# Mixture-of-experts feed-forward on one core: own rows fetched apart from the gathers, one-hots in 16 bits, packed sizes, five visits, an end by block

## The reference, cut to what matters

```python
x_rot = cond(x)                          # gate and rotation, linear
top1 = argmax(softmax(x_rot @ router_w + router_b))
for i in range(8):
    a, g = split(x_rot @ w1[i] + b1[i])  # 256 -> 2 x 1024
    y = (a * sigmoid(g)) @ w2[i] + b2[i] # 1024 -> 256
    out = out + where(top1 == i, y, 0)
return x + out
```

## Time and profile before

| | us |
|---|---|
| median of 3 runs | 209.33 (209.0 to 209.66) |
| the profiled execution, its own time | 207.35 |
| its span, first to last instruction | 205.6 |
| mean granted TensorE clock | 0.994 of full |
| busy: PE, DVE, ACT, POOL | 191.6, 146.1, 125.1, 87.7 |
| moved by DMA | 42.34 MB |

### The profile page before, as it was taken

The page is one execution under the profiler, slowest core; times in us unless marked ns, Lnnn a source line. Parts: engine busy times, 40 slices in busy tenths (PEclk is TensorE's granted clock), DMA queues, the critical chain, the costliest instruction groups (busy, mean ns, idle before and its releaser), DMA issues.

```text
span 205.6 us, 4304 instructions
## 1 busy us (share of the span) xinstructions
PE 191.6 (93%) x1451; PEld 181.2 (88%) x1453; DVE 146.1 (71%) x296; ACT 125.1 (61%) x222; POOL 87.7 (43%) x138
## 2 busy tenths in 40 slices
PE   7997867999999999999999999999999999999960
PEld 3777733999999999999999999999999999999950
DVE  4928944678854888398869869995999488839510
ACT  2454770385756676486875958695777667648310
POOL 8002544631700645445467084555637364004403
PEclk9999999999999999999999999999999999999997
DMA  4999925879948161787198469618861976001001
GB/s 136 383 402 385 311 64 190 261 260 328 308 128 357 51 213 47 249 333 238 34 390 302 154 199 406 232 38 303 344 205 53 336 277 208 0 0 37 28 5 43
DMA packets 20054, 42.34 MB, mean 206 GB/s; under 512 B 2472, under 2 KB 14905, under 8 KB 17978
## 3 DMA queue, kind: packets, MB, share of 16 engines
q1 hardware_dynamic: 15808, 31.54, 42.8%
q0 software_dynamic: 4000, 10.50, 16.1%
q10 hardware_dynamic: 218, 0.01, 0.1%
HBM read 35.74 MB, written 8.13 MB: 213 GB/s over the span
## 4 chain that ended last, share of the span: by engine, by line
PE 90%; DMA 4%; issue 1%; DVE 1%; POOL 1%; ACT 1%; DVEq 0%; POOLq 0%
PE y_ps L1208 8%; PE g_ps L1176 8%; PE g_ps L1169 8%; PE a_ps L1169 8%; PE y_ps L1210 8%; PE a_ps L1176 8%; PE y_ps L1209 8%; PE a_ps L1172 8%; PE g_ps L1172 8%; PE y_ps L1120 3%; PE y_ps L942 3%; DMA x_turn<-x_rows,g_idx 2%; PE a_ps L1018 2%; PE a_ps L1099 2%; DMA x_rows<-arena 2%
## 5 line engine op out<-in xcount | busy, mean ns | idle before, releaser
L854 DVE SCALAR_TENSOR_TENSOR arena<-a_ps,b_t,arena 128x336 f32<-128x336 f32 (+1 forms) x64 | 33.3, 521 | 27.7 <-PE a_ps L1176 24.1
L579 ACT ACTIVATE arena<-g_ps,b_t 128x336 f32<-128x336 f32 (+1 forms) x64 | 32.2, 503 | 32.4 <-PE g_ps L1176 32.2
L452 POOL DMA_INDIRECT out_dram<-x_turn,s_idx x22 | 28.5, 1295 | 47.3 <-DVE x_turn L874 35.4
L740 DVE TENSOR_TENSOR w_lo<-w_raw,w_hi 128x1024 fp32r<-128x1024 f32 x32 | 37.7, 1221 | 9.1 <-DMA x_turn<-x_rows,g_idx 5.2
L438 POOL DMA_INDIRECT x_turn<-x_rows,g_idx x24 | 30.6, 1275 | 31.1 <-DMA out_dram<-x_turn,s_idx 17.3
L1208 PE MATMUL y_ps<-u_hi,w_hi 128*128 128x336 f32 (+2 forms) x128 | 38.1, 298 | 0.3 <-issue 0.3
L1210 PE MATMUL y_ps<-u_lo,w_hi 128*128 128x336 f32 (+2 forms) x128 | 37.5, 293 | 0.0
L1209 PE MATMUL y_ps<-u_hi,w_lo 128*128 128x336 f32 (+2 forms) x128 | 37.5, 293 | 0.0
L1169 PE MATMUL g_ps<-xr_hi,w_hi 128*128 128x336 f32 (+2 forms) x128 | 36.1, 299 | 0.0
L1169 PE MATMUL a_ps<-xr_hi,w_hi 128*128 128x336 f32 (+2 forms) x128 | 35.6, 294 | 0.0
L1172 PE MATMUL a_ps<-xr_hi,w_lo 128*128 128x336 f32 (+2 forms) x128 | 35.5, 293 | 0.0
(11 more groups left out here) (181 smaller groups left out, 306.8 us busy)
## 6 DMA issues: line engine op xcount, KB each, us to landing
w_raw<-in_L_ffn_w_dram SPq DMA_DIRECT2D x16, 1024.0 KB, 7.9
w_raw<-in_L_ffn_w_dram SPq DMA_DIRECT2D x16, 512.0 KB, 4.6
x_own<-in_x_dram SPq DMA_DIRECT2D x4, 512.0 KB, 6.0
x_rows<-x_own SPq DMA_DIRECT2D x4, 512.0 KB, 11.1
x_rows<-arena SPq DMA_DIRECT2D x8, 256.0 KB, 3.4
x_turn<-x_rows,g_idx POOLq DMA_INDIRECT x24, 6.0
out_dram<-x_turn,s_idx POOLq DMA_INDIRECT x22, 3.7
x_own<-x_rows,g_idx POOLq DMA_INDIRECT x8, 5.6
```

The lines of the kernel that those rows point to most:

```text
L579: nc.scalar.activation(sig[:, c % SIG_RING, 0:n], pair[c % RING][1][:, 0:n], ACT.Sigmoid, bias=b1_t[:, bass.ds(e * (2 * NC) + (NC + c), 1) ...
L740: V.tensor_tensor(unit_of(w1_lo, u), raw_unit(u), unit_of(w1_hi[:, :].bitcast(F32), u), ALU.subtract)\
L854: V.scalar_tensor_tensor(u32[:, c % (8 - SIG_RING), 0:n], pair[c % RING][0][:, 0:n], b1_t[:, bass.ds(e * (2 * NC) + c, 1)], sig[:, c % SIG ...
```

## The change

Six things are changed together.

- `x_rows` keeps only the rotated tokens (rows of 256 numbers). The four copies of `x` into it go. Each sub-tile is now filled by two indirect DMAs: `gather` takes the rotated row, and `fetch` takes the token's own row from the input. `gather(i+1)` no longer waits for the scatter of tile i-2; `fetch(i+1)` comes behind `scatter(i-1)` and has that wait.
- The slot one-hots are made by two 16-bit operations over 8 tokens each, with the token innermost, in place of 16 small ones; the token's number moves from them to the sub-tile one-hots, which take two operations each. POOL makes the table `steps16` for it.
- The sizes of all tiles lie in one word, `packed`, ready before `ctrl`; PE reads that word alone before the first tile.
- PE's order: the router's weights are turned behind f = 6, not f = 4; `rotate_blocks(2)` stands ahead of the wait for `in_row`; five visits in place of six, at other places.
- At the end PE turns back the first half of the features while ACT works on the second, whose first 128 columns come apart; the second half is turned back block by block into four banks, and DVE adds it so.
- DVE's first split of `w1` waits for the first gathered sub-tile, not for two.

```diff
-    x_rows = nc.dram_tensor("x_rows", (TOK, 2 * DIM), F32, kind="Internal").ap()
+    x_rows = nc.dram_tensor("x_rows", (TOK, DIM), F32, kind="Internal").ap()
@@ sync
-            for g in range(4):
-                sp.wait_ge(x_loaded[g], 16)
-                sp.dma_start(x_rows_v[:, 4 * g:4 * g + 4, DIM:ROW], x_tok[:, 4 * g:4 * g + 4, :]).then_inc(x_part_written, 16)
@@ gpsimd
+            nc.gpsimd.iota(steps16[:, :, :], pattern=[[1, P], [0, NB]], base=0, channel_multiplier=0,
+                           allow_small_or_imprecise_dtypes=True).then_inc(steps16_set, 1)
...
-                        out=pairs[buffer_of(i)][:, s * ROW:(s + 1) * ROW], out_offset=None, in_=x_rows,
+                        out=pairs[buffer_of(i)][:, s * ROW:s * ROW + DIM], out_offset=None, in_=x_rows,
...
+            def fetch(i):
+                for s in range(NSUB):
+                    nc.gpsimd.indirect_dma_start(
+                        out=pairs[buffer_of(i)][:, s * ROW + DIM:(s + 1) * ROW], out_offset=None, in_=x_flat,
+                        in_offset=bass.IndirectOffsetOnAxis(ap=g_idx[:, i * NSUB + s:i * NSUB + s + 1], axis=0),
+                        bounds_check=row_bound, oob_is_err=False).then_inc(fetched, 16)
...
             for i in range(NE):
                 wait_gathered(i)
                 if i + 1 < NE:
-                    if i + 1 >= YB:
-                        wait_scattered(i + 1 - YB)
                     gather(i + 1)
                 else:
                     nc.gpsimd.drain()
                 if i > 0:
                     scatter(i - 1)
                 else:
+                    fetch(0)
+                if i + 1 < NE:
+                    if i + 1 >= YB:
+                        wait_scattered(i + 1 - YB)
+                    wait_fetched(i)
+                    fetch(i + 1)
@@ scalar
                 if i >= NE - 1:
-                    for h in range(KH):
-                        biased(i, e, h, 0, FIRST, yt_done[h])
+                    biased(i, e, 0, 0, min(n, FIRST), yt_done[0])
+                    biased(i, e, 1, 0, P, yt_first)
+                    biased(i, e, 1, P, min(n, FIRST), yt_done[1])
@@ vector
+            def slot_one_hots(half):
+                tokens = slice(half * NB // 2, (half + 1) * NB // 2)
+                V.tensor_tensor(slot_oh[:, :, tokens], steps16[:, :, tokens],
+                                r_16[:, tokens].unsqueeze(1).to_broadcast([P, P, NB // 2]), ALU.is_equal).then_inc(slots_ready, 1)
...
+                link(V.tensor_tensor(to, steps16[:, first:first + count, :],
+                                     at[:, :].unsqueeze(1).to_broadcast([P, count, NB]), ALU.is_equal))
+                return V.tensor_tensor(to, to, tok_16[:, :].unsqueeze(1).to_broadcast([P, count, NB]), ALU.mult)
...
+            V.tensor_scalar(packed[:, :], left, float(len(SIZES) * sum(PLACES)), None, ALU.add).then_inc(packed_ready, 1)
...
+                V.tensor_tensor(rows[:, 0:blocks, 0], y_half[0][:, 0:blocks * P].rearrange("p (s d) -> p s d", d=P),
+                                rows[:, 0:blocks, 0], ALU.add)
+                for s in range(blocks):
+                    dve.wait_ge(block_turned, (i - NE + 1) * NSUB + s + 1)
+                    last = V.tensor_tensor(rows[:, s, 1], apart[s][:, 0:P], rows[:, s, 1], ALU.add)
...
-            for s in range(2):
-                dve.wait_ge(gathered[s], 16)
+            dve.wait_ge(gathered[0], 16)
@@ tensor
+            visit(2)
             keep_warm(early_ps, 5)
...
             rotate_blocks(1)
+            rotate_blocks(2)
+            visit(4)
             pe.wait_ge(consts_ready, CONSTS)
             pe.wait_ge(in_row_ready, 1)
...
-            visit(5)
             pe.wait_ge(still32_set, 1)
...
             last.then_inc(idx_spare_summed, 1)
+            visit(5)
             keep_warm_long(late_ps, 2)
-            pe.wait_ge(ctrl_ready, 1)
-            last_tile = load_last(pe)
-            visit(6)
-            keep_warm_long(late_ps, 2)
-            LANDING_AT = {(0, 7): 3, (1, 2): 4, (2, 3): 6}
+            pe.wait_ge(packed_ready, 1)
+            LANDING_AT = {(0, 2): 2, (1, 6): 4, (2, 1): 5}
+            LANDING_BEHIND = {0: 3}
...
-            turn_back_rows(NSUB)
+            pe.wait_ge(yt_done[0], at1)
+            for s in range(NSUB):
+                last = T.transpose(y_half[0][:, s * P:(s + 1) * P], yt[:, s * P:(s + 1) * P], ident[:, :])
+            last.then_inc(half_turned, 1)
+            for s in range(NSUB):
+                if s < 2:
+                    pe.wait_ge((yt_first, yt_done[1])[s], at1)
+                T.transpose(apart[s][:, 0:P], yt[:, ITEM + s * P:ITEM + (s + 1) * P], ident[:, :]).then_inc(block_turned, 1)
```

More of the change, by code:

```diff
@@ L55, in adaln_moe_ffn_kernel @@
     LEFT = 3
-    SPECIAL = len(SIZES)
+    PLACES = [1 << (LEFT * e) for e in range(NE)]
     EPS = 1e-8
@@ L105, in adaln_moe_ffn_kernel @@
         s_idx = sb("s_idx", TAB * NSUB, I32)
-        ctrl = sb("ctrl", 3 + TAB, I32)
+        ctrl = sb("ctrl", 2 + TAB, I32)
+        packed = sb("packed", 1, I32)
+        places = sb("places", NE)
         ident = sb("ident", P)
@@ L500, in _ @@
                         gather(i)
+                        fetch(i)
                         scatter(i)
@@ L833, in _ @@
             V.tensor_scalar(ctrl[:, 1 + NE:1 + TAB], owner, float(MORE), None, ALU.add)
-            V.memset(ctrl[:, 1 + TAB:2 + TAB], 0)
-            link(V.tensor_tensor(places[:, :], places[:, :], steps, ALU.mult))
-            link(V.tensor_reduce(left, places[:, :], AX.X, ALU.add))
-            V.tensor_scalar(ctrl[:, 2 + TAB:3 + TAB], left, float(SPECIAL << (LEFT * (NE - 1))), None, ALU.add)\
-                .then_inc(ctrl_ready, 1)
+            V.memset(ctrl[:, 1 + TAB:2 + TAB], 0).then_inc(ctrl_ready, 1)
             dve.wait_ge(idx_spare_summed, 1)
@@ L985, in _ @@
                 if f == 3:
-                    visit(2)
-                if f == 4:
+                    visit(3)
+                if f == 6:
                     pe.wait_ge(wr_loaded, 16)
@@ L1035, in _ @@
             T.matmul(xk_ps[1][:, NE:2 * NE], ones16[:, :], in_row[:, :], start=True, stop=True).then_inc(ranks_ready, 1)
-            for b in range(2, NB // 2):
+            for b in range(GROUPS - 1, NB // 2):
                 rotate_blocks(b)
-                if b == 5:
-                    visit(4)
             pe.wait_ge(b1_loaded, 16)
@@ L1233, in leaf, with jump, by_size @@
                 second_half(size, 1)
-            def by_size(size, low, high):
-                if low == high:
-                    if low == SPECIAL - 1:
-                        with pe.If(size >= SPECIAL):
-                            here = nc.cur_bb
-                            pe.br("special")
-                            nc.switch_bb("behind_special", parent=here)
+            def jump(to, behind):
+                here = nc.cur_bb
+                pe.br(to)
+                nc.switch_bb(behind, parent=here)
+            def by_size(code, low, high):
+                if low == high:
                     leaf(low)
@@ L1248, in by_size @@
                 middle = (low + high + 1) // 2
-                with pe.If(size < middle):
-                    by_size(size, low, middle - 1)
+                with pe.If(code > len(SIZES) - middle):
+                    by_size(code, low, middle - 1)
                 with pe.Else():
-                    by_size(size, middle, high)
+                    if middle == high == len(SIZES) - 1:
+                        with pe.If(code < 1):
+                            jump("special", "behind_special")
+                    by_size(code, middle, high)
             begin = nc.cur_bb
```

132 lines of the change are left out of this document (70 added, 62 removed).

## The result

The changed kernel took 206.06 us in the median of four runs against 209.17 us for the kernel before on the same chip: a ratio of 0.9851, 95% interval 0.9807 to 0.9894, or 3.1 us less. Forecast were 207.0 us and a range from 206.0 to 208.8.

A forecast was written before the change was run, and what follows sets the result against it. PE alone was taken to bound 36 to 192 us, the head waiting for rotated rows in DRAM and the end being single steps. -0.9 - 0.15 - 0.3 - 1.0 = -2.35 took 209.33 to 207.0 us, range 206.0 to 208.8.

The forecast's parts named there:

- Rotation order, -0.9: Head: rotate_blocks(2) fits into PE's wait for in_row, so the last write to x_rows comes 0.9 us earlier.
- Copies of x gone, -0.15: Head: without four copies on SP's queue the last x_rows write lands 0.15 us sooner, bounds 0 and 0.4.
- Half as wide gathers, -0.3: First gather: half the bytes per sub-tile bring the first product 0.3 us sooner, bounds 0 and -0.4.
- 16-bit one-hots, 0: Head: g_idx stays ready before the last x_rows write lands, so the new one-hots change nothing, 0 us.
- Rival 5: Head: strided one-hot reads make the index last, 0.2 to 1 us too late; 207.5 us, chance 0.04.
- `packed`, visits, filling products, 0: Head: all this lies before the gather lands, so shorter preparation buys nothing; PE rests longer, 0 us.
- rival 4: Before the first gather: PE's longer rest drops its clock to 1.2 GHz, costing about 2 us; 209, chance 0.04.
- Visits, 0: Head: PE's five visits, counted among the work before the gather lands, were put at 0 us.
- rival 3: First tile: five visits may leave a PE instruction block unfetched, about 1.5 us; 208.5 us, chance 0.05.
- First split, `fetch`, 0: Tiles: earlier w1 split gains nothing; added fetch issues nearly fill POOL but cause no stall at gather(4), 0 us.
- rival 1: Fourth tile: gather(4)'s third sub-tile still takes 7.9 us, PE stands 1.5 us; 208.5 us, chance 0.11.
- End by block, -1.0: End: turning back half during ACT's work, then by block, starts POOL's scatter 1.0 us sooner; 0.4 if PE comes late.

The follow-up runs named there:

- e3: Changed kernel with the third rotation, rotate_blocks(2), put behind the rank products again; 208.26 us, ratio 0.9966 to the kernel before.
- e11: e8 with the edit of e3 (rotation behind the rank products again); 205.22 us, ratio 0.9828 to the kernel before.
- e1: Changed kernel measured and profiled again, no edit; 207.82 us, ratio 0.9900 to the kernel before.
- e8: Changed kernel with visit(3) behind f = 7 and two more filling products in PE's rest; 203.43 us, ratio 0.9761 to the kernel before.
- e10: e8 with the four copies of x to DRAM put back, POOL waiting for them; 205.36 us, ratio 0.9845 to the kernel before.
- e2: Changed kernel with the four copies of x put back into an unread tensor, POOL waiting for them; 208.19 us, ratio 0.9911 to the kernel before.
- e7: Changed kernel with two more filling products right behind the index products, in PE's rest; 206.21 us, ratio 0.9865 to the kernel before.
- e12: e8 with the end of the kernel before; 204.33 us, ratio 0.9783 to the kernel before.
- e4: Changed kernel with the end of the kernel before; 207.71 us, ratio 0.9983 to the kernel before.
- first profile: First profiled execution of the changed kernel, no edit, with a long rest of PE in the head; 209.34 us.
- e5: Changed kernel with visit(3) behind f = 7 instead of f = 3; 206.50 us, ratio 0.9875 to the kernel before.
- e6: Changed kernel without the two filling products behind visit(5); 206.91 us, ratio 0.9908 to the kernel before.

## Why the prediction was right, point by point

- **Rotation order, -0.9: right.** Argmax to last write is 8.54 and 8.53 us in the two profiles of the kernel before and in e3 and e11, 7.65 in e1 and e8, 7.71 in e10: -0.83 to -0.89.
- **Copies of x gone, -0.15: mis-sized.** The step took its bound from the fastest write of the kernel before, 2.9 us, as if that were the floor. With the copies gone and the rows narrower, the writes land in 2.0 to 2.3 us in the median, and in 3.4 before. Writes and POOL's delay together brought 1.6 us (4.18 from last write to gather in the earlier trace rows, 2.60 in e1). e10 gives 1.0 of it back by the copies and the wait for them (0.64 in the landing, 0.28 in POOL's delay). The other 0.6 goes with something that the step left out: `x_rows` is now half as wide, so a partition's two rows lie together. The packets show it. DMA view of the kernel before, in the stretch of the last write (24 to 28.5 us):

```profile
DMA packets 863, 0.84 MB, mean 187 GB/s; under 512 B 58, under 2 KB 862, under 8 KB 862
```

  The same view of e8, 23.4 to 26.5 us:

```profile
DMA packets 367, 0.65 MB, mean 211 GB/s; under 512 B 48, under 2 KB 48, under 8 KB 367
```

  Nearly all packets were under 2 KB before; now only the 48 smallest are. That this is the reason was not tried by itself; the writes with the copies beside them, 2.7 to 2.8 us in the median with dense rows (e2, e10) and 3.4 without (both profiles before), speak for it.
- **Half as wide gathers, -0.3: fits.** Where the clock is at 1.00 the first product follows the gather's issue by 6.99 to 7.40 us (e7, e8, e10, e11, e12), against 7.68 and 7.92 in the two profiles of the kernel before. Where PE's weight load waits for the third sub-tile, that has landed 3.28 us after the start of its issue in e8 and 3.17 in e10, against 3.71 and 4.10 in the kernel before. No run separated it.
- **16-bit one-hots, 0: right, with less margin.** In e1 `g_idx` is written by 25.88 us and the write lands about 26.2. Rival 5 did not occur; the sixteen index products take 1.25 us (1.08 before).
- **`packed`, visits, filling products, 0: the step that failed.** It reasoned that all of this lies before the gather lands and so hides. It named a longer rest, but placed it behind the spare products. It is in front of them: DVE now writes the counts for `packed` before the spare one-hots, which PE waits for until 28.07 (in e7 and e8, where less rest is left, the profile names `q_oh_spare` as what ends it). The rest of 2.42 us, against 0.99 before, is rival 4's mechanism, which had 0.04: the clock fell, and fillers that had been hidden became the chain. The price was about 2 us (9.25 against 7.21 in e8), as that rival said, and 1.3 to 1.6 in e2, e3 and e4 (8.54, 8.76 and 8.85), where the low clock did not last as long; the time did not go to its 209 because other terms gave more than forecast.
- **Visits, 0: wrong too.** This is rival 3's mechanism in another place: it looked for a stall at the first tile, and it came in the head. In four of seven profiles with `visit(3)` at f = 3, PE stood 1.8 to 3.2 us behind it, until 2.8 us after a block had moved on the instruction queue; in none of the five with the visit at f = 7. There PE still waited up to 1.66 us, but for the load of `x`.
- **First split, `fetch`, 0: the mechanism of rival 1, in small.** The middle is 0.4 us longer (161.7 to 161.9 us in eleven profiles, 161.3 in both of before), just inside the 0.5 that was set as its mark; in the first profile it is 162.3, beyond it. The loss sits where the prediction saw its tightest place, at `gather(4)` in the fourth tile: in all twelve profiles of the changed kernel and its variants PE's weight load waits there for the gather, and in none of the two before. Timelines of e1 and, behind it, of the first profile:

```profile
111.99 0.14 PEld L1133 LDWEIGHTS a_ps<-ident,x_turn 128*128 128x128 f32 x1 [0.33 <-DMA x_turn<-x_rows,g_idx]
```

```profile
115.61 0.33 PE L1133 MATMUL a_ps<-ident,x_turn 128*128 128x128 f32 x1 [0.52 <-DMA x_turn<-x_rows,g_idx]
```

  It is the second sub-tile that comes late, not the third: issued at 104.25 in e1, it landed 7.71 us later (in the first profile issued at 107.45, about 8.1 later), close to the 7.9 of the earlier trace rows though its rows are half as long. The step took no stall because it looked at the third alone, which was to land at 111.2; the second landed at 111.96.
- **End by block, -1.0: right**, -1.14 to -1.17.
- **Sums.** The upper bound of -1.3 keeps the whole 0.9 of the rotations; with the 0 that the prediction itself gives as their bound it is -0.4 (208.9); POOL's 15.6 + 2.1 + 1.7 are 19.4 us, not 19.2; and an index that has 1.7 us to spare has 0.65 once the write comes 1.05 earlier, not 0.8 to 0.9. Nothing in the outcome hangs on them.
- **Not forecast: the tail.** From the first scatter to the end of the span it is 5.5 and 5.4 us in the kernel before, and 4.0 to 4.5 in all twelve profiles of the changed one and its variants, with the old end (4.0 in e4 and e12) and the copies (4.35 and 4.5) too. So about 1.2 us belong to the change and, for the most part, to neither of these parts; which part, and by what way, stays open.

In sum: unforeseen gains (1.5 in the write, 1.2 in the tail) and unforeseen losses (2.0 in the clock, 0.4 in the middle, and up to 3 at `visit(3)`) nearly cancelled. That they did is luck: the total was right, near the low end of its range, and the working behind it was right for the rotations, the end and the indices alone.

## What to carry to other kernels

When a wait in front of a tensor engine gets longer, look at the granted clock behind it before calling it hidden: filling products sized for the old waits become work on the path, at double time. Put them inside the rest, not behind it. When a transfer gets smaller neighbours or a denser layout, don't take its fastest time in the old trace as its floor. And a jump made only to have code fetched early belongs where nothing is waiting, since it can wait for the fetch itself. Where transfers are laid out one behind the other to find a late one, each piece that a product needs is compared with its own deadline, not the last piece alone.

## What the hardware showed that I had not expected

- The length of a rest did not decide alone what the clock did. The rest of 2.42 us in front of the spare products was followed by a clock of 0.50 to 0.56 over the next 6 us in the first profile, e1, e5 and e6, but by 0.72 in e2, e3 and e4. Of the pauses among the turns of `x`, 2.02 us (first profile) and 3.17 us (e4) were followed by 0.60 and 0.62, while 2.82 us (e3), 1.79 us (e2) and 1.66 us (e12) left it at 1.00. Windows of e3 and of e4 behind their pauses:

```profile
12.30:16.00 3.70, 3.65 (x40) 3.03 (x44) 1.02 (x4) 1.58 (x3) 0.00 (x0) 1.00 0.60 250
```

```profile
13.30:17.00 3.70, 3.68 (x20) 3.60 (x20) 0.17 (x1) 1.79 (x3) 0.00 (x0) 0.62 0.34 142
```

  From the end of the pause to the first logits the same products took 2.51 us in e3 and 3.71 in e4, so the clock added 1.2 us to a head that was already late. No run tried to separate what tips it.
- PE, behind a jump ahead, went on 2.76 to 2.81 us after the start of a 16 KB block on the instruction queue, in six profiles in which that block moved between 7.64 and 10.52 us. While it waited, the DMA engines were full (a share of 1.02 from 10.2 to 13.3 us in e4).
- A write of 256 KB to DRAM took 3.4 us in the median as rows 1 KB long two kilobytes apart beside four 512 KB writes, 2.7 to 2.8 as pairs of rows lying together beside the same writes, and 2.0 to 2.3 without them, though the four had been issued before it. A write issued after the four had landed took 2.0 beside them too (the last one of e2).
- Loads of `x` issued within 2.9 us of each other landed after 4.3 to 9.4 us from one execution to the next, and the argmax, the same work in all, came between 15.74 and 20.60 us, the latest behind `visit(3)`. A good part of the scatter of the timed runs is made there.
